# Graph propagation with the counts as weights: groups of 128 slots summed by a 0/1 matrix in place of blocks of 512 summed by a scan

## The reference

```
layer 1:  for _ in range(3):  x = segment_sum(x[src], dst) / max(count, 1);   final += x / 4
layer 3:  for _ in range(3):  x = segment_sum(norm * x[src], dst);            acc += x;   result acc / 4
          norm = rsqrt(deg)[src] * rsqrt(deg)[dst]
```

## Time and profile before

| | |
|---|---|
| median of three runs (lowest, highest) | 15430.6 us (15423.8, 15435.31) |
| span of the profiled execution | 14066.3 us |
| what lies around the span, as median less span | 1364.3 us |
| TensorE busy | 9466.4 us, 67% |
| VectorE busy | 8214.5 us, 58% |
| ScalarE busy | 6584.2 us, 47% |
| GpSimd busy | 8729.6 us, 62% |
| instructions | 164878 |
| granted TensorE clock, mean | 0.718 |

### The profile page before, as it was taken

How to read it: one execution, slowest core, us unless ns; L and a number is a source line. 1 busy time by engine, 2 the same in 40 slices (tenths; PEclk the granted TensorE clock), 3 DMA queues, 4 the chain that set the end, 5 groups by cost and what they waited for, 6 DMA issues and landing times. The chain is left out here.

```text
span 14066.3 us, 164878 instructions
## 1 busy us (share of the span) xinstructions
PE 9466.4 (67%) x47732; PEld 6096.5 (43%) x47732; DVE 8214.5 (58%) x5617; ACT 6584.2 (47%) x6430; POOL 8729.6 (62%) x7438
## 2 busy tenths in 40 slices
PE   2355555555555552999998477767767674999998
PEld 2244444444444442555554233333333332555555
DVE  2366666666666666787877233333333333778877
ACT  1244444444444443888886122222222221888887
POOL 5777777777777776232324777777777776142323
PEclk7555555555555555999999666666666665999999
DMA  5233333333333332999998233333333332999998
GB/s 88 48 89 86 89 86 89 86 89 86 89 87 88 87 88 70 311 296 312 294 312 243 49 65 65 65 65 65 65 65 65 65 64 44 312 301 305 295 312 259
DMA packets 3238421, 1981.98 MB, mean 141 GB/s; under 512 B 1212287, under 2 KB 3140913, under 8 KB 3238257
## 3 DMA queue, kind: packets, MB, share of 16 engines
q1 hardware_dynamic: 2785457, 1664.63, 41.5%
q0 software_dynamic: 239424, 185.44, 7.5%
q10 hardware_dynamic: 213504, 131.51, 3.3%
HBM read 1602.28 MB, written 381.54 MB: 141 GB/s over the span
## 5 line engine op out<-in xcount | busy, mean ns | idle before, releaser
L624 POOL DMA_INDIRECT attend_and_count_rows<-table,attend_and_count_ring x3136 | 3917.4, 1249 | 1029.6 <-issue 1002.7
L1230 POOL DMA_INDIRECT judge_edges_rows<-table,judge_edges_ring x3128 | 2951.6, 944 | 1013.5 <-issue 988.6
L1133 POOL DMA_INDIRECT base<-slot_sums,last_slot x588 | 1273.2, 2165 | 2914.7 <-DMA slot_sums<-propagate_mean_out 1364.4
L659 PE MATMUL attend_and_count_counts<-attend_and_count_hot_hi,attend_and_count_hot_lo 128*128 128x98 bf16 x15680 | 1377.0, 264 | 2377.5 <-ACT attend_and_count_stage L769 1501.9
L1340 DVE TENSOR_TENSOR_SCAN judge_edges_feat<-judge_edges_keep,judge_edges_feat,judge_edges_p_feat 32x512 f32<-32x512 bf16 x782 | 960.1, 1265 | 2495.6 <-PE judge_edges_p_feat L1284 2474.3
L659 PEld LDWEIGHTS attend_and_count_counts<-attend_and_count_hot_hi,attend_and_count_hot_lo 128*128 128x128 bf16 x15680 | 1154.9, 130 | 2598.6 <-ACT attend_and_count_stage L769 1626.6
L1039 PE MATMUL propagate_mean_p_dense<-propagate_mean_part,propagate_mean_split 128*96 128x512 bf16 x9114 | 1994.3, 380 | 199.3 <-ACT propagate_mean_part L966 174.8
L1039 PE MATMUL propagate_norm_p_dense<-propagate_norm_part,propagate_norm_split 128*96 128x512 bf16 x9114 | 1992.8, 380 | 188.7 <-ACT propagate_norm_part L966 158.6
L966 ACT CAST propagate_norm_part<-propagate_norm_raw 128x7168 bf16<-128x7168 uint8 x282 | 1720.0, 6162 | 337.8 <-DVE propagate_norm_slot_sum L1088 296.1
L966 ACT CAST propagate_mean_part<-propagate_mean_raw 128x7168 bf16<-128x7168 uint8 x282 | 1720.0, 6162 | 336.7 <-DVE propagate_mean_slot_sum L1088 295.3
L687 DVE TENSOR_TENSOR attend_and_count_hot_hi<-ramp_hi,attend_and_count_key_hi 128x3136 bf16<-128x3136 bf16 x490 | 878.0, 1792 | 1359.8 <-ACT attend_and_count_key_lo L737 1349.0
(11 more groups left out here) (236 smaller groups left out, 10196.0 us busy)
## 6 DMA issues: line engine op xcount, KB each, us to landing
propagate_mean_raw<-matrix SPq DMA_DIRECT2D x651, 896.0 KB, 6.5
propagate_norm_raw<-matrix SPq DMA_DIRECT2D x651, 896.0 KB, 6.5
matrix<-attend_and_count_stage SPq DMA_DIRECT2D x245, 784.0 KB, 3.9
scan<-attend_and_count_out SPq DMA_DIRECT2D x784, 68.0 KB
inject<-attend_and_count_zeros SPq DMA_DIRECT2D x196, 256.0 KB, 2.0
attend_and_count_rows<-table,attend_and_count_ring POOLq DMA_INDIRECT x3136
judge_edges_rows<-table,judge_edges_ring POOLq DMA_INDIRECT x3128
judge_edges_rows<-inject SPq DMA_DIRECT2D x782, 64.0 KB
```

What stands on the lines that cost most here:

```text
L624: nc.gpsimd.indirect_dma_start(out=rows[:, u, g, j, :], out_offset=None, in_=D.table0[:, :], in_offset=rows_of(ring[:, u, g, j:j + 1])).th ...
L659: last = nc.tensor.matmul(counts[:, r % 2, k // 4, NH * (k % 4):NH * (k % 4) + NH], hot_lo[:, u, slot, :], hot_hi[:, u, slot, :], start=Tr ...
L1133: nc.gpsimd.indirect_dma_start(out=sums[:, h, :], out_offset=None, in_=D.slot_sums[0:blocks * BLOCK, :], in_offset=rows_of(S.last_slot[:, ...
L1230: nc.gpsimd.indirect_dma_start(out=rows[:, u, half, j, 0:FEAT], out_offset=None, in_=D.table2[:, :], in_offset=rows_of(ring[:, u, half, j: ...
```

## The change

The roles in the matmul are exchanged. The counts of a **group** of 128 slots become the weights (128 x 128 bf16, one load for each of the 98 columns), the split features `split[:, h]` (96 columns) move, and the result stands with slots on partitions: `p_dense` is 128 x 96 for each of 124 groups, four PSUM banks in turn. The layout in DRAM is one run of 6272 bytes per partition and 64 slots, and SyncE loads a whole group (128 x 2 x 6272 bytes) at once, into four buffers. The cast of a group is in two sides, columns 0 to 38 on ScalarE and 39 to 97 on VectorE, and turns the order from (pair, column, slot) to (column, slot). The round's split has the same two sides.

In place of scan, carry and transposes: `prepare_slots_and_nodes` stores the node of every slot as rows (`D.node_rows`, rotated by one place, so that column 0 is the group's last slot; a further word says whether the group begins a new node). Per group VectorE compares that row, broadcast to 128 partitions, with the node of its own partition's slot (`S.node_col`), which gives a 0/1 matrix `mask`; it adds the three bf16 parts (128 x 96 to 128 x 32), adds the carried sum of the previous group to row 0, and TensorE multiplies mask and sums in f32 (`spread_sums`). Every slot then holds its node's whole sum in the group, with the group's last slot on partition 0. ScalarE copies it out of PSUM (`keep_sums`) and, once in four groups, stores it. Since the stored order differs, `prepare_ends` works out the new row of a node's last slot.

```diff
-PLACE = (0, 1, 2, 3, 4, 2, 3)
-SPLIT_PART = 4
+GROUP = P
+N_GROUPS = SLOTS // GROUP
+GROUP_PAIRS = GROUP // PAIR
+SPLIT_AT = 39
+SIDES = (slice(0, SPLIT_AT), slice(SPLIT_AT, NH))
+RAW_BUFFERS = LANES
+ROW_WORDS = GROUP + 4
...
 (prepare_slots_and_nodes, vector)
+            dve.wait_ge(numbered, 1)
+            link(nc.vector.memset(node_row[:, P:], 0.0))
+            nc.vector.tensor_copy(node_row[:, P:P + 1], flags_f[:, 0, 0:1])
+            nc.vector.tensor_tensor(node_row[:, 1:P], slot_row[:, 0:P - 1], whole[:, 0:P - 1], ALU.subtract)
+            marks["node_row"] = link(nc.vector.tensor_tensor(node_row[:, 0:1], ...))
...
+            link(nc.vector.tensor_copy(S.node_col[:], node_of[:]))
...
 (prepare_ends, vector: one copy becomes seven small operations)
-            link(nc.vector.tensor_copy(S.last_slot[:], own[:, :, 0]))
+            link(nc.vector.tensor_scalar(place[:, 0], own[:, :, 0], BLOCK - 1, None, ALU.bitwise_and))
...
 (propagate)
+    def widen(eng, copy, k, b, u, q):
+        _, uses, pairs = place_of(k, b, u)
+        side = SIDES[q]
+        eng.wait_ge(multiplied[q][u % 2], pairs)
+        eng.wait_ge(loaded[u], uses * 32 + 32)
+        copy(part[:, u % 2, side].rearrange("p h (s v) -> p s h v", v=PAIR),
+             raw[:, u, :, side.start * PAIR:side.stop * PAIR].rearrange("p s (h v) -> p s h v", v=PAIR)).then_inc(widened[q][u], 1)
...
 (sync)
+                        for q in range(len(SIDES)):
+                            sp.wait_ge(widened[q][u], uses)
+                        sp.wait_ge(carried[u], uses)
+                        sp.dma_start(raw[:, u], D.matrix[...]).then_inc(loaded[u], 16)
+                        sp.dma_start(rows[:, u], D.node_rows[...].to_broadcast([P, ROW_WORDS])).then_inc(loaded[u], 16)
...
 (scalar)
+            def keep_sums(k, b, u):
+                n, blocks, _ = place_of(k, b, u)
+                if u == 0:
+                    act.wait_ge(stored, blocks * 16)
+                act.wait_ge(spread, n + 1)
+                nc.scalar.copy(whole[:, u], p_whole[:, u, 0:FEAT]).then_inc(kept, 1)
+                if u == LANES - 1:
+                    act.wait_ge(kept, n + 1)
+                    act.dma_start(D.slot_sums[...], whole[:].rearrange("p j f -> p (j f)")).then_inc(stored, 16)
+            def one(k, b, u, leads, is_last):
+                if not is_last:
+                    widen(act, nc.scalar.copy, k, *next_of(b, u), 0)
+                if not leads:
+                    keep_sums(k, *((b, u - 1) if u else (b - 1, LANES - 1)))
...
 (tensor)
+            def spread_sums(k, b, u):
+                n, uses, _ = place_of(k, b, u)
+                pe.wait_ge(S.tables_done, 1)
+                pe.wait_ge(carried[u], uses + 1)
+                nc.tensor.matmul(p_whole[:, u, 0:FEAT], mask[:, u % 2], added[:, u % 2], start=True, stop=True).then_inc(spread, 1)
+            def one(k, b, u, leads, is_last):
+                for q, side in enumerate(SIDES):
+                    if leads:
+                        pe.wait_ge(splitted, k * 2 + (q + 1))
+                    pe.wait_ge(widened[q][u], uses + 1)
+                    for h in range(side.start, side.stop):
+                        last = nc.tensor.matmul(p_dense[:, u, 0:3 * FEAT], part[:, u % 2, h], split[:, h].rearrange("p c f -> p (c f)"),
                                                 start=(h == 0), stop=(h == NH - 1))
+                    last.then_inc(multiplied[q][u % 2], 1)
                     if q == 0 and not leads:
+                        spread_sums(k, *((b, u - 1) if u else (b - 1, LANES - 1)))
...
 (vector)
+            def add_group(k, b, u):
+                dve.wait_ge(loaded[u], uses * 32 + 32)
+                nc.vector.tensor_scalar(mask[:, u % 2], rows[:, u, 0:GROUP], S.node_col[:, column], None, ALU.is_equal)
+                dve.wait_ge(multiplied[len(SIDES) - 1][u % 2], pairs + 1)
+                nc.vector.tensor_reduce(added[:, u % 2], p_dense[:, u, 0:3 * FEAT].rearrange("p (c f) -> p f c", c=3),
+                                        AX.X, ALU.add).then_inc(summed_parts, 1)
+                dve.wait_ge(summed_parts, n + 1)
+                dve.wait_ge(kept, n)
+                nc.vector.scalar_tensor_tensor(added[0:1, u % 2], whole[0:1, (u - 1) % LANES], rows[0:1, u, GROUP:GROUP + 1],
+                                               added[0:1, u % 2], ALU.mult, ALU.add).then_inc(carried[u], 1)
+            def one(k, b, u, leads, is_last):
+                if not is_last:
+                    widen(dve, nc.vector.tensor_copy, k, *next_of(b, u), 1)
+                add_group(k, b, u)
```

More of the change, by code:

```diff
@@ L941, in propagate @@
     sums = scaled = S.square = S.base
[L942 to L951 removed]
+    p_dense = pb("p_dense", [P, RAW_BUFFERS, 512], f32)
@@ L1064, in _ @@
                 link(nc.vector.tensor_tensor(scaled[:], S.x[:], over_features(before[:]), ALU.mult))
-            for side in sides:
+            for side in SIDES:
                 split_x(side, link)
```

183 lines of the change are left out of this document (80 added, 103 removed).

## The result

The changed kernel takes 15284.8 us (median of 4 runs, 15274.4 to 15308.4) against 15427.2 us of the kernel before on the same chip (4 runs, 15419.6 to 15435.3): ratio 0.9913, 95% interval 0.9899 to 0.9927. It is faster, by 142 us or 0.9%; forecast were 296. The time lies inside the range of 15000 to 15550, and inside the band of 15020 to 15320 that was held the likeliest.

What follows compares the result with a forecast made beforehand. TensorE was taken to bound the old kernel, VectorE the new at 4.87 us a group, p = 4.95. Stages -153 and -146.5 with preparation +3.5 gave -296, from 15430.6 to 15135 us; range 15000 to 15550.

Steps and rivals of the forecast that it cites:

- TensorE, 4.8 a group: TensorE's work per group: 98 matmuls at 47.5 ns and the f32 product of mask and sums, 4.8 us.
- VectorE, 4.87: VectorE's work per group: cast 4.03, mask 0.21, reduction 0.30, carry 0.25, loop end 0.08, together 4.87 us.
- ScalarE, 4.74: ScalarE's work per group: cast 4.27, copy out of PSUM 0.19, a share of store issue and loop end, 4.74 us.
- The loads: DMA per group: 1.67 MB in 4.1 to 4.95 us, issued three groups ahead, landing in 6.5, ScalarE's wait absorbed.
- p: Time of one group, from carry to carry inside a round: forecast 4.95 us, ends 4.75 and 5.5.
- Start and rounds' ends: Before a stage's first carry 27 us (norm 28.7); each round's end 26 us beyond one p (norm 29).
- Preparation, +3.5: Small added operations for the new slot order and `last_slot`, and a store only SyncE waits for: +3.5 us.
- 2: Rival 2: DMA at 311 GB/s needs 5.38 us per group, so no change, 15454 us; chance 0.08.
- 1: Rival 1: row 0's carry waits for ScalarE's copy behind its cast, p = 5.8, 15765 us; chance 0.09.
- 3: Rival 3: TensorE's 98 small matmuls run at half-clock pace, 8.5 us per group, 17770 us; chance 0.04.
- 4: Rival 4: VectorE's turned cast runs at one element per cycle, p = 8.85, 18030 us; chance 0.03.
- 5: Rival 5: GpSimd's gathers, locked out by VectorE's casts, take two groups each, +495 us in each of six rounds; chance 0.04.

Runs made afterwards that it cites:

- e3: The early kernel: changed kernel with counts loaded once both casts have read the buffer, node rows on their own semaphore one group later; ratio 0.9799 to the unchanged kernel.
- e10: e7 with the loops over blocks unrolled twice on TensorE, VectorE and ScalarE; ratio 0.9698 to the unchanged kernel.
- e2: Changed kernel with the second half of every group's counts not loaded, zeros instead, so not the layer's result; ratio 0.9732 to the unchanged kernel.
- e6: e3 with sides of 40 and 58 columns instead of 39 and 59; ratio 0.9780 to the unchanged kernel.
- e7: e3 with sides of 40 and 58 columns and ScalarE's wait for the store moved just ahead of the next store; ratio 0.9739 to the unchanged kernel.
- e12: The changed kernel itself run again, on another chip; ratio 0.9927 to the unchanged kernel there (15594 us).
- e14: e3 run again on the same chip as e12; ratio 0.9794 to the unchanged kernel there (15594 us).
- e8: e3 without the 0/1 matrix made per group, ones instead, so not the layer's result; ratio 0.9771 to the unchanged kernel.
- e11: e3 with half of each group's counts not loaded and no 0/1 matrix per group, so not the layer's result; ratio 0.9722 to the unchanged kernel.
- e4: Changed kernel with sides of 40 and 58 columns instead of 39 and 59; ratio 0.9914 to the unchanged kernel.
- e1: The unchanged kernel timed and profiled again on another chip, nothing altered; 15578 us.
- e15: e7 run again on the same chip as e12; ratio 0.9737 to the unchanged kernel there (15594 us).

## Why the prediction fell short

The step that failed is the cover which the prediction assumed for the loads. Its terms in their order:

- **TensorE, 4.8 a group: held.** 98 matmuls in 4.33 us (44 ns each) and a product of 0.37 (0.28 forecast). The rows' 47.5 ns was near. The Trainium skill's "TensorE: Matmul & The Clock Gate", section "Back-to-back issue gap", states some 81 ns per pair at 128 columns; this trace, with 96 columns and 44 ns, does not agree.
- **VectorE, 4.87: a little too high.** The shortest turns are 4.64, and one in four has 0.41 of loop end (in e3 a block's first turn is 5.08, its third 4.67): 4.74.
- **ScalarE, 4.74: its own work held** (cast 4.35, copy 0.19). That its copy would wait for the store of the block before was not in the sum: 45.1 us in the mean propagation, 56 times. A store took 4.8 us to land in the kernel before and takes 7.4 in e10 (medians). That the loads delay it fits e2, where half of them are gone and the wait with them; whether it is their place ahead in the queues or the shared rate is open. It decides once the loads are in time (e6 to e7).
- **The loads: the step that failed.** "Landing takes some 6.5, and two overlap, so ScalarE's wait of under 1 us is absorbed." The 6.5 was that of the old, smaller loads; the new ones took 9.3 us to their use. ScalarE asked for the load shown above 8.5 us after its issue and not 5.7, so that its wait was indeed under 1 us (0.59 in the mean over 372 casts), but it was not absorbed: 221 us of idle time before ScalarE's casts and 66 before VectorE's, in the mean propagation, end with a load, and p was 5.15 instead of 4.95. That is 738 x 0.20 = 148 us, nearly the whole miss. With the counts on a semaphore of their own and issued at the earliest moment, p is 4.89, under the forecast: the cover assumed for the loads was not there. Two things were overlooked in the code: the casts wait for a small second transfer behind the large one, and the large one waits for a carry that does not concern its buffer. Each costs about half (e12 to e14). That 4.89 is so near the sum over the engines is in part luck: VectorE's term was 0.13 too high, ScalarE's wait for its store was not in it, and e8 and e11 show the early kernel bound by the transfer as well.
- **Start and rounds' ends: 20 us too small.** 34.0 a round's end against 31 (norm 37.2 against 34), a start 30.3 against 27 (norm 32.9 against 28.7). The split casts at about half speed account for it: 1.45 and 2.12 us with 39 and 59 columns, 0.83 and 1.13 with 40 and 58. The Trainium skill, "VectorE: DVE Perf Modes", section "What auto-detection actually checks", asks for outermost dimensions of source and destination that are both even or equal, if a cast is to take two elements per cycle; these rows agree. The prediction priced it at 29 us and left it out; measured are 4.9 us a split, 29 in six, and by e4's four round ends and two starts 12.6 + 9.9 = 22 of them on the path.
- **Preparation, +3.5:** not to be told from nothing (`prepare_ends` starts at 544.5 in e1, at 540.8 and 544.5 in e4 and e3 on the same chip; its own operations last 6.9 instead of 5.3 us).
- **The sum** by these: -299.5 + 148 + 20 = -131 for the stages, measured -136; the 4 left are not accounted for.
- **Rivals.** 2 (the loads bound it anyway) was the nearest: the turn lay between it (5.38) and the forecast. 1 showed only in a small part: VectorE waited 43.6 us in 71 of 372 carries for ScalarE. 3 and 4 did not come. Neither did 5 in this kernel, where no gather took over 4.9 us, but without the mask one in four took two casts (e11).

The best kernel tried is e10, at 0.9698 of the unchanged one (0.9685 to 0.9712). Open stay what makes the stages beside the propagations slower on most chips, what a register-found column costs by itself, and how much of e10's lead over e7 is the chip: e7 and e15 agree on two chips, but e10's chip is a third.

## What to carry to other kernels

Where one engine bounds a stage, the transfers are covered by its time; a change that shortens it takes that cover away. So write down for each load the earliest moment at which its buffer is free, the moment at which it is issued, and how many transfers are queued ahead of it, not the landing time of the old kernel's smaller transfers. Tie a large transfer's semaphore to nothing but its own readers, and a small one's to its own. Where three engines and the queues stand within some per cent, single repairs look worthless and pay only together.

## What was not expected of the hardware

- One program takes 14068 us on one chip and 15427 to 15594 on the others, most of it in the judging stage (3970 to 3975 against 5151 to 5242 us), some in the attention (4954 to 4956 against 4977 to 5114) and in what lies before and behind it, none in the unchanged kernel's propagations.
- A gather on GpSimd took 0.94 us with VectorE idle and some 4.5 (at most 4.9) under VectorE's back-to-back casts, one per cast; in the mean over the changed kernel's 588 it took 3.88, before 2.17. With the mask left out, 142 of 588 (e11) and 72 of 588 (e8) took 8 to 8.7 us.
- The 16 DMA engines, at a share of 0.94 to 0.97, moved 329 to 348 GB/s with 6272-byte runs, the higher figures where the next load is always queued.
